# Layer 2 of a four-layer attention kernel: exponentials turned before they are normalised, the context product with tokens on partitions and a column of ones

## The chip, the core and the metric

One core of a Trainium2 chip. The time is the device time of one execution in microseconds (us). TensorE is PE (its weight loads are PEld), VectorE DVE, ScalarE ACT, GpSimd POOL.

## The reference

Four cross-attention layers follow each other on x and a context, both (32, 64, 256) in float32. The change is in layer 2, grouped-query attention with 32 query heads on 8 key/value heads of 8 features:

```
q = x @ Wq + bq ; k = ctx @ Wk + bk ; v = ctx @ Wv + bv      # 32 heads of q, 8 of k and v, HD = 8
attn = softmax(q @ k.T / sqrt(8) + mask)                      # (32 batches, 32 heads, 64, 64)
x = (attn @ v) @ Wo + bo + x                                  # then a layer norm
```

## The kernel before

2048 tokens are worked on as PAIRS = 16 pairs of batches, 128 tokens each. Layers 0 and 1 come first, then `phase_mlp_grouped_attention`: the MLP of layer 1 and, behind it, layer 2's attention, one pair after another. Layer 3 follows behind a barrier. Every engine has its own in-order queue, written out by hand as a loop over t in which several pairs are in flight; `there(p)` leaves out pairs that don't exist, and semaphores join the queues.

A pair's scores lie on 128 partitions (2 of the query heads times 64 query tokens), 2048 in each (16 heads, 2 batches, 64 keys), in two halves of 1024. Its way:

- PE `project(p)` (products through `accumulate`, L1322): queries, keys and values into one PSUM bank. ACT `move_projected` copies queries (L1493) and values (L1498), the latter into `v_bd`, which has zeros around them; DVE `place_keys` (L1577) spreads the keys.
- PE `scores(p)` (L1385). DVE `add_mask(p, half)`: scale and mask out of PSUM into `soft` (L1554), row maxima (L1561). POOL `subtract(p, half)` (L1282). ACT `exponent(p, half)` (L1479).
- DVE `invert(p, half)`: sums (L1565) and their reciprocals (L1570). POOL `normalize(p, half)` multiplies into `prob` (L1290, two instructions a half).
- PE `turn(p, half)`: 8 transposes into `t_ps` (L1398). `t_ps` has room for one half, so that the second half waits for ACT `move_turned(p, 0)` (L1483), which copies it to `pt`.
- PE `context(p)` (L1410): 16 products. `v_bd` is the stationary side with 32 columns, `pt` the moving side with 128; four products at a time go to the four column strips of the array. The result has features on partitions. ACT `move_context` (L1507).
- PE `outputs(p)`: two products with Wo (L1418) and one of a row of ones with the bias (L1419). DVE `add_output` (L1582) adds onto x.

A float32 product makes two weight-load and two matmul records in the trace, a transpose one of each. Queue orders of one step t: PE scores(t-1), project(t), context(t-3), turn(t-2, 0), outputs(t-3), turn(t-2, 1). ACT exponent(t-2, 1), move_projected(t), move_context(t-3), move_turned(t-2, 0), exponent(t-1, 0), move_turned(t-2, 1). At t = 2 also `turn_features(LAST)` (L1360, moved at L1474), which turns the last block of the MLP's result. The full orders are in the loops below.

Of the kernel before, what the change touches and what calls it, by code (L numbers as in the profile page):

```python
# [1203 lines left out]
def phase_mlp_grouped_attention(nc, A, G, w, b1, g, loads, loads3):  # L1204
# [14 lines left out]
    with Mem(nc, "mg", G.psum) as m:  # L1219
# [6 lines left out]
        cols, bv_wide, one = m.sb("cols", [P, 4]), m.sb("bv_wide", [P, P]), m.sb("one", [1, P])  # L1226
# [6 lines left out]
        rmax, rsum, rinv = (m.sb(n, [P, HALVES, 16]) for n in ("rmax", "rsum", "rinv"))  # L1233
# [5 lines left out]
        s_ps, t_ps = m.ps("s_ps", (P, TILES, 4, 2, T)), m.ps("t_ps", (P, 2, 2, 2, P))  # L1239
        p_bank, c_bank = m.ps("p_bank"), m.ps("c_bank")  # L1240
        hid_ps = [s_ps[:, n, :, :, :].rearrange("p v b t -> p (v b t)") for n in range(RING)]
        out_ps = [t_ps[:, n, :, :, :].rearrange("p b q n -> p (b q n)") for n in range(2)]
        q_ps, k_ps, v_ps = p_bank[:, 0:D].rearrange("p (c n) -> p c n", c=2), p_bank[:, D:D + P], p_bank[:, D + P:D + P + 64]
        c_ps, o_ps = c_bank[:, 0:D].rearrange("p (b c t) -> p b c t", b=2, c=2), c_bank[:, 0:D]
# [7 lines left out]
        zero_made, v_zero, folded_made, spread_made, one_made = (m.sem(n) for n in ("zero_made", "v_zero", "folded_made", "spread_made", "one_made"))  # L1252
# [3 lines left out]
        s_psum, masked, max_done, shifted, exp_done, sum_done, inv_done, prob_ready = (m.sem(n) for n in  # L1256
            ("s_psum", "masked", "max_done", "shifted", "exp_done", "sum_done", "inv_done", "prob_ready"))
        t_psum, pt_done, c_psum, ot_done, o_psum, x_done = (m.sem(n) for n in
            ("t_psum", "pt_done", "c_psum", "ot_done", "o_psum", "x_done"))

        def there(pair):
            return 0 <= pair < PAIRS
# [4 lines left out]
        with nc.Block() as block:  # L1267
# [10 lines left out]
            def _(pool):  # L1278
# [5 lines left out]
                def normalize(p, half):  # L1284
                    pool.wait_ge(inv_done, 2 * p + half + 1)
                    if p:
                        pool.wait_ge(t_psum, 2 * p + half - 1)
                    for n in range(2):
                        i = 2 * half + n
                        pool.tensor_tensor(prob[:, i, :, :, :].rearrange("p b v t -> p v b t"), soft[p % 2][half][:, n, :, :, :],  # L1290
                                           rinv[:, half, 8 * n:8 * n + 8].rearrange("p (v b) -> p v b", v=4).unsqueeze(3)
                                           .to_broadcast([P, 4, 2, T]), ALU.mult).then_inc(prob_ready, 1)
# [4 lines left out]
                pool.memset(v_bd[:, :, :, :, :], 0.0).then_inc(v_zero, 1)  # L1297
                pool.memset(one[:, :], 1.0).then_inc(one_made, 1)
# [9 lines left out]
                for t in range(PAIRS + 2):  # L1308
                    if there(t - 2):
                        normalize(t - 2, 0)  # L1310
                    if there(t - 1):
                        subtract(t - 1, 0)
                    if there(t - 2):
                        normalize(t - 2, 1)
                    if there(t - 1):
                        subtract(t - 1, 1)

            @block.tensor
            def _(pe):
# [43 lines left out]
                def project(p):  # L1363
# [25 lines left out]
                def turn(p, half):  # L1389
                    pe.wait_ge(prob_ready, 4 * p + 2 * half + 2)  # L1390
# [4 lines left out]
                    for n in range(2):  # L1395
                        for b in range(2):
                            for q in range(2):
                                mm = pe.transpose(t_ps[:, n, b, q, :],  # L1398
# [814 lines left out]
```

## Time and profile before

| | |
|---|---|
| median of 3 runs | 1658.1 us (1653.25 to 1659.24) |
| the profiled execution | 1658.67 us, its span 1656.9 us |
| busy: PE, PEld, DVE, ACT, POOL | 1541.7, 1321.7, 1102.9, 673.1, 451.4 us |
| scores of pair 0 and of pair 15 start | 1192.45 and 1325.93 us |

The span is from the first to the last instruction. Line numbers in the rows are those of the kernel before. A row of the timeline has start, duration (both us), engine, line, instruction, what it writes and reads, how many are merged, and in brackets the idle time ahead of it with what ended it.

### The profile page before, as it was taken

To read this page: it belongs to the slowest core of one execution; us is meant where nothing else is said; L and a number is where in the kernel's file an instruction comes from. 1 tells how busy PE (TensorE), PEld (TensorE's weight loads), DVE (VectorE), ACT (ScalarE), POOL (GpSimd) and SP (SyncE) were. 2 spreads that over 40 slices of the span, in tenths; PEclk is the share of its full clock that TensorE was granted. 3 is DMA by queue.
4 is the path that set the end of the run, shared out by engine and by line. 5 is a ranking of instruction groups with operands and counts; after the bars stand their busy time and mean duration, and the time that the engine had idled before them with its cause. 6 is when DMAs were issued, how large, how long until landed. Compare 5 with 4: busy or idle time off the path is not lost. (4 is left out here: it accounts for less than half of the span.)

```text
span 1656.9 us, 33073 instructions
## 1 busy us (share of the span) xinstructions
PE 1541.7 (93%) x13299; PEld 1321.7 (80%) x13299; DVE 1102.9 (67%) x2371; ACT 673.1 (41%) x1270; POOL 451.4 (27%) x532
## 2 busy tenths in 40 slices
PE   4987999999999999999999999879988859999799
PEld 2666888888888888888888888869867747888598
DVE  6886666666666676666666667555599945676444
ACT  4654434343333434433343434432366633544322
POOL 2004120020101211210200200232188866653211
PEclk9998999999999999999999999889989979999899
DMA  4000010010000000000100100020030000000000
GB/s 132 1 0 26 14 39 14 1 39 14 27 14 14 27 14 14 27 14 14 39 14 1 39 27 1 30 45 1 2 115 2 1 1 2 2 2 3 1 26 25
DMA packets 44580, 34.16 MB, mean 21 GB/s; under 512 B 10770, under 2 KB 41496, under 8 KB 44312
## 3 DMA queue, kind: packets, MB, share of 16 engines
q1 hardware_dynamic: 44440, 32.17, 6.7%
q8 instruction: 102, 1.67, 0.4%
q14 instruction: 38, 0.31, 0.1%
HBM read 30.00 MB, written 2.10 MB: 19 GB/s over the span
## 5 line engine op out<-in xcount | busy, mean ns | idle before, releaser
L946 DVE STREAM_TRANSPOSE att_pt<-att_prob 32x256 f32<-32x256 f32 x496 | 215.9, 435 | 6.4
L846 ACT ACTIVATE g_q_sb<-psum,g_cols 128x512 f32<-128x512 f32 x128 | 88.4, 690 | 321.0 <-PE psum L714 321.0
L763 PE MATMUL psum<-g_wo_hi,att_ot_hi 128*128 128x256 f32 x512 | 150.2, 293 | 2.5 <-DVE att_ot_lo L959 1.4
L917 DVE TENSOR_REDUCE att_rmax<-psum 128x6 f32<-128x390 f32 (+1 forms) x96 | 49.2, 512 | 151.3 <-PE psum L676 151.3
L763 PE MATMUL psum<-g_wo_lo,att_ot_hi 128*128 128x256 f32 x512 | 145.5, 284 | 0.0
L763 PE MATMUL psum<-g_wo_hi,att_ot_lo 128*128 128x256 f32 x512 | 145.4, 284 | 0.0
L746 PE MATMUL psum<-att_pt,att_v_sb 128*128 128x128 f32 x1024 | 128.9, 280 | 3.5 <-DVE att_ot_lo L959 3.5
L969 DVE TENSOR_TENSOR g_x_res<-psum,g_x_res 128x256 f32<-128x256 f32 x128 | 54.3, 424 | 116.8 <-PE psum L763 88.5
L746 PEld LDWEIGHTS psum<-att_pt,att_v_sb 128*128 128x128 f32 x1024 | 123.2, 194 | 7.8 <-DVE att_ot_lo L959 3.7
L849 ACT ACTIVATE att_k_sb<-psum,g_cols 128x512 f32<-128x512 f32 x128 | 88.2, 689 | 81.0 <-PE psum L714 81.0
L714 PE MATMUL psum<-split_feat_hi,g_wide_hi 128*128 128x512 f32 x256 | 103.7, 405 | 4.5 <-DVE split_feat_lo L993 3.3
L728 PE MATMUL psum<-g_wv_hi,split_ctx_hi 128*128 128x512 f32 x256 | 105.6, 413 | 0.0
L763 PEld LDWEIGHTS psum<-g_wo_hi,att_ot_hi 128*128 128x128 f32 x512 | 98.7, 193 | 5.1 <-DVE att_ot_lo L959 1.7
L714 PE MATMUL psum<-split_feat_lo,g_wide_hi 128*128 128x512 f32 x256 | 100.6, 393 | 0.0
L714 PE MATMUL psum<-split_feat_hi,g_wide_lo 128*128 128x512 f32 x256 | 100.4, 392 | 0.0
L763 PEld LDWEIGHTS psum<-g_wo_lo,att_ot_hi 128*128 128x128 f32 x512 | 98.8, 193 | 1.9
L728 PE MATMUL psum<-g_wv_hi,split_ctx_lo 128*128 128x512 f32 x256 | 100.0, 391 | 0.0
L728 PE MATMUL psum<-g_wv_lo,split_ctx_hi 128*128 128x512 f32 x256 | 99.9, 390 | 0.0
L829 ACT ACTIVATE att_ot_hi<-psum 128x512 fp32r<-128x512 f32 x128 | 73.3, 593 | 65.5 <-PE psum L746 65.5
L714 PE MATMUL psum<-split_ctx_hi,g_wide_hi 128*128 128x512 f32 x256 | 99.9, 390 | 0.0
L714 PE MATMUL psum<-split_ctx_lo,g_wide_hi 128*128 128x512 f32 x256 | 99.8, 390 | 0.0
L714 PE MATMUL psum<-split_ctx_hi,g_wide_lo 128*128 128x512 f32 x256 | 99.8, 390 | 0.0
(301 smaller groups left out, 3936.5 us busy)
## 6 DMA issues: line engine op xcount, KB each, us to landing
g_ctx_f<-in_L_xattn_wq SPq DMA_DIRECT2D x32, 128.0 KB, 2.3
g_ctx_f<-in_L_xattn_wk SPq DMA_DIRECT2D x32, 128.0 KB, 2.8
g_ctx_f<-in_L_xattn_wv SPq DMA_DIRECT2D x8, 512.0 KB, 3.8
g_ctx_f<-in_L_xattn_wo SPq DMA_DIRECT2D x8, 512.0 KB, 3.8
c_ctx_tok<-in_ctx SPq DMA_DIRECT2D x4, 512.0 KB, 5.5
g_x_res<-in_x SPq DMA_DIRECT2D x4, 512.0 KB, 8.7
g_w<-in_L_xattn_mlp_w SPq DMA_DIRECT2D x2, 1024.0 KB
out<-g_x_res SPq DMA_DIRECT2D x8, 256.0 KB, 2.2
```

Source lines behind the costliest of these rows:

```text
L714: mm = pe.matmul(dst[:, :], a, b_, start=(k == 0 and t == 0), stop=(k == KT - 1 and t == 2))
L728: mm = pe.matmul(v_ps[p % 2][:, :], a, b, start=(k == 0 and t == 0), stop=(k == KT - 1 and t == 2))
L746: mm = pe.matmul(c_ps[:, p % 2, h, :], v_sb[:, p, h * K1:(h + 1) * K1], pt[:, h, pp, p % 2, :, :].rearrange("p u t -> p (u t)"), start=Tru ...
L763: mm = pe.matmul(o_ps[p % 2], a, b, start=(h == 0 and t == 0), stop=(not last and h == HG - 1 and t == 2))
L829: act.activation(ot_hi[:, p, :, :], c_ps[:, p % 2, :, :], ACT.Copy).then_inc(ot_high, 1)
L846: act.activation(q_sb[:, h, :], q_ps[:, :], ACT.Identity, bias=G.cols[:, layer, head:head + 1]).then_inc(q_ready, 1)
L849: act.activation(k_sb[:, h, :, 0:T], k_ps[:, :].rearrange("p (b t) -> p b t", t=T), ACT.Identity, bias=G.cols[:, layer, H1 + head:H1 + hea ...
L917: dve.tensor_reduce(rmax[:, a:b], s_ps[group][:, :, :], X_AXIS, ALU.max).then_inc(max_done, 1)
L946: turned = dve.transpose(pt[to:to + 32, :, :, r, u, 32 * a:32 * a + 32].rearrange("p h a t -> p (h a) t"), by_pair[of:of + 32, :, u, 32 * ...
L969: dve.tensor_tensor(G.x_res[:, pair, :], o_ps[p % 2], G.x_res[:, pair, :], ALU.add).then_inc(x_added, 1)
```

## The change

The division by the sums moves from the 2048 probabilities of a partition to the 256 context values. `exponent` is followed by `turn` directly. `context(p)` has `pt` (128 columns) as the stationary side and as the moving side the values of both batches with a column of ones behind each, 2 x 9 = 18 columns; 16 products, none side by side in the array, with query tokens on partitions. DVE `normalize` inverts the sums (columns 8) and multiplies while it leaves PSUM; `turn_context` turns the result so that features are on partitions; `outputs` has two products, and POOL adds the bias onto x beforehand. `prob`, `one`, the sums' instructions and POOL's multiplications go. Context moves a step earlier, behind `turn(t-2, 1)`, and outputs last. The same in short:

```diff
-    v_bd = m.sb("v_bd", [P, 4, 2, 2, 2 * ROWS])
-    prob = m.sb("prob", [P, TILES, 2, 4, T])
+    v_bd = m.sb("v_bd", [P, 4, 8, 2, HD + 1])
+    ctx_n = m.sb("ctx_n", [P, 2, 16, HD])
...
-    c_ps, o_ps = c_bank[:, 0:D].rearrange("p (b c t) -> p b c t", b=2, c=2), c_bank[:, 0:D]
+    c_ps = c_bank[:, 0:2 * 16 * (HD + 1)].rearrange("p (b h d) -> p b h d", b=2, h=16)
+    ct_ps, o_ps = c_bank[:, 0:D].rearrange("p (b c t) -> p b c t", b=2, c=2), p_bank[:, 0:D]
...
+            def add_bias(p):
+                pool.tensor_tensor(G.x_res[:, p, :], G.x_res[:, p, :], g.o_bias[:, :], ALU.add).then_inc(bias_added, 1)
...
+            pool.wait_ge(bias_done, 1)
+            pool.wait_ge(f_psum, KT * NBLK)
+            pool.wait_ge(mlp_done, 2 * NBLK)
+            for p in range(PAIRS):
+                subtract(p, 0)
+                add_bias(p)
+                subtract(p, 1)
...
                 if p:
                     pe.wait_ge(k_done, p)
+                if p >= 4:
+                    pe.wait_ge(x_done, p - 3)
...
             def turn(p, half):
-                pe.wait_ge(prob_ready, 4 * p + 2 * half + 2)
+                pe.wait_ge(exp_done, 2 * p + half + 1)
...
+                    for v in range(4):
+                        mm = pe.transpose(t_ps[:, n, v, :], soft[p % 2][half][:, n, v, :, :].rearrange("p b t -> p (b t)"), G.ident[:, :])

             def context(p):
                 pe.wait_ge(pt_done, 2 * p + 2)
                 pe.wait_ge(v_done, p + 1)
                 if p:
-                    pe.wait_ge(x_done, p)
+                    pe.wait_ge(ot_done, p)
+                for i in range(TILES):
+                    for v in range(4):
+                        mm = pe.matmul(c_ps[:, :, 4 * i + v, :], pt[:, p % 2, i, v, :], v_bd[:, p % 4, 4 * (i % 2) + v, :, :],
+                                       start=True, stop=True)
+                mm.then_inc(c_psum, 1)
+
+            def turn_context(p):
+                pe.wait_ge(norm_done, p + 1)
                 for b in range(2):
+                    mm = pe.transpose(ct_ps[:, b, :, :].rearrange("p c t -> p (c t)"), ctx_n[:, b, :, :].rearrange("p h d -> p (h d)"), G.ident[:, :])
+                mm.then_inc(ct_psum, 1)
 
             def outputs(p):
                 pe.wait_ge(ot_done, p + 1)
-                for c in range(2):
-                    pe.matmul(o_ps, ot[:, c, :], g.wo[:, c, :], start=(c == 0), stop=False)
-                pe.matmul(o_ps, one[:, :], g.o_bias[0:1, :], start=False, stop=True).then_inc(o_psum, 1)
+                pe.wait_ge(k_done, min(p + 4, PAIRS))
+                accumulate(o_ps, [(ot[:, c, :], g.wo[:, c, :]) for c in range(KT)]).then_inc(o_psum, 1)
...
-                if there(t - 3):
-                    context(t - 3)
                 if there(t - 2):
                     turn(t - 2, 0)
                 if there(t - 3):
-                    outputs(t - 3)
+                    turn_context(t - 3)
                 if there(t - 2):
                     turn(t - 2, 1)
+                    context(t - 2)
+                if there(t - 3):
+                    outputs(t - 3)
...
             def move_turned(p, half):
                 act.wait_ge(t_psum, 2 * p + half + 1)
+                if p >= 2:
+                    act.wait_ge(c_psum, p - 1)
+                act.activation(pt[:, p % 2, tiles(half), :, :].rearrange("p i v n -> p (i v n)"),
+                               t_ps[:, :, :, :].rearrange("p i v n -> p (i v n)"), ACT.Copy).then_inc(pt_done, 1)
...
                 for b in range(2):
-                    for u in range(2):
-                        a = act.activation(
-                            v_bd[T * u:T * u + T, p % 4, b, :, :].rearrange("p h (q x) -> p h q x", x=16)[:, :, 0:4:3, 8 * u:8 * u + 8],
-                            v_ps[T * b:T * b + T, :].rearrange("p (h q u d) -> p h q u d", h=2, q=2, u=2)[:, :, :, u, :], ACT.Copy)
+                    a = act.activation(v_bd[T * b:T * b + T, p % 4, :, b, 0:HD],
+                                       v_ps[T * b:T * b + T, :].rearrange("p (h d) -> p h d", h=8), ACT.Copy)
...
                 if t == 2:
                     move_features(LAST)
+                if there(t - 2):
+                    move_turned(t - 2, 0)
                 if there(t - 3):
                     move_context(t - 3)
-                if there(t - 2):
-                    move_turned(t - 2, 0)
                 if there(t - 1):
                     exponent(t - 1, 0)
                 if there(t - 2):
...
-                    dve.wait_ge(prob_ready, 4 * (p - 2) + 2 * half + 2)
+                    dve.wait_ge(t_psum, 2 * (p - 2) + half + 1)
...
+            def normalize(p):
+                dve.wait_ge(c_psum, p + 1)
                 if p:
+                    dve.wait_ge(ct_psum, p)
+                dve.reciprocal(rinv[:, :, :], c_ps[:, :, :, HD]).then_inc(inv_done, 1)
+                dve.wait_ge(inv_done, p + 1)
+                dve.tensor_tensor(ctx_n[:, :, :, :], c_ps[:, :, :, 0:HD], rinv[:, :, :].unsqueeze(3).to_broadcast([P, 2, 16, HD]),
+                                  ALU.mult).then_inc(norm_done, 1)
...
             def add_output(p):
                 dve.wait_ge(o_psum, p + 1)
+                dve.wait_ge(bias_added, p + 1)
                 dve.tensor_tensor(G.x_res[:, p, :], o_ps, G.x_res[:, p, :], ALU.add).then_inc(x_done, 1)
...
             for t in range(1, PAIRS + 3):
+                if there(t - 3):
+                    normalize(t - 3)
                 if there(t - 1):
                     add_mask(t - 1, 0)
-                if there(t - 2):
-                    invert(t - 2, 1)
-                if there(t - 1):
                     add_mask(t - 1, 1)
                 if t == 1:
                     add_block(LAST)
                 if t >= 2 and there(t):
                     place_keys(t)
-                if there(t - 1):
-                    invert(t - 1, 0)
                 if there(t - 3):
                     add_output(t - 3)
```

## Rows read from the trace of the kernel before

**Rows 1.** The page, part 1: busy time and share of the span.
```profile
PE 1541.7 (93%) x13299; PEld 1321.7 (80%) x13299; DVE 1102.9 (67%) x2371; ACT 673.1 (41%) x1270; POOL 451.4 (27%) x532
```
**Rows 2.** Busy time by stretch, layer 2's attention: stretch, length, engines, clock share, DMA.
```profile
1209.50:1325.90 116.40, 104.93 (x1119) 83.20 (x1118) 108.78 (x129) 72.73 (x143) 100.76 (x78) 0.95 0.08 23
1325.90:1348.10 22.20, 16.03 (x163) 11.64 (x162) 11.13 (x16) 9.22 (x11) 12.67 (x11) 0.85 0.01 2
1272.60:1307.70 35.10, 30.72 (x349) 24.36 (x348) 33.82 (x41) 22.38 (x44) 31.33 (x25) 1.00 0.01 2
```
**Rows 3.** Timeline, one step of the loop at full clock.
```profile
1245.90 1.15 PE L1385 MATMUL psum<-mg_k_bd,mg_q_sb 32*128 32x256 f32 x16
1246.97 1.16 PE L1322 MATMUL psum<-split_feat_f,mg_wq 128*128 128x128 f32 x8
1247.11 1.23 DVE L1554 SCALAR_TENSOR_TENSOR split_soft<-psum,mg_mask 128x1024 f32<-128x1024 f32 x1 [0.18 <-PE psum L1385]
1248.37 1.22 DVE L1561 TENSOR_REDUCE mg_rmax<-split_soft 128x16 f32<-128x1024 f32 x1
1248.90 1.08 PE L1410 MATMUL psum<-split_pt,mg_v_bd 128*32 128x128 f32 x32
1249.67 1.90 POOL L1282 TENSOR_TENSOR split_soft<-split_soft,mg_rmax 128x1024 f32<-128x1024 f32 x1 [0.90 <-DVE mg_rmax L1561]
1249.91 1.09 PE L1398 MATMUL psum<-g_ident,mg_prob 128*128 128x128 f32 x8
1250.84 1.07 PE L1418 MATMUL psum<-g_wo,mg_ot 128*128 128x256 f32 x4
1251.84 0.69 PE L1419 MATMUL psum<-g_o_bias,mg_one 1*128 1x256 f32 x2
1253.63 1.09 PE L1398 MATMUL psum<-g_ident,mg_prob 128*128 128x128 f32 x8 [1.10 <-POOL mg_prob L1290]
```
**Rows 4.** Timeline, a turn at half clock, its move and the exponentials behind it.
```profile
1204.13 1.94 PE L1398 MATMUL psum<-g_ident,mg_prob 128*128 128x128 f32 x8 [2.68 <-ACT split_feat_f L1474]
1206.11 1.02 ACT L1483 ACTIVATE split_pt<-psum 128x1024 f32<-128x1024 f32 x1 [2.12 <-PE psum L1398]
1207.03 1.05 ACT L1479 ACTIVATE split_soft<-split_soft 128x1024 f32<-128x1024 f32 x1
```
**Rows 5.** Weight loads and narrow products, by line and in the timeline.
```profile
L1901 PEld LDWEIGHTS psum<-l_v_one,l_pt x1024: 132/138/138, 1385.6 to 1547.8; 128*64 128x64 f32 x171
L1418 PEld LDWEIGHTS psum<-g_wo,mg_ot x64: 186/190/337, 1215.0 to 1346.4; 128*128 128x128 f32 x64
...
1248.31 0.53 PEld L1322 LDWEIGHTS psum<-g_wkv,g_ctx_f 128*128 128x128 f32 x4
...
1406.76 2.00 PE L1901 MATMUL psum<-l_v_one,l_pt 128*64 128x17 f32 x64
```
**Rows 6.** By line: what goes, and layer 3's instructions of the kind that comes.
```profile
L1565 DVE TENSOR_REDUCE mg_rsum<-split_soft x32: 1206/1209/1221, 1199.7 to 1337.6; 128x16 f32<-128x1024 f32 x32
L1290 POOL TENSOR_TENSOR mg_prob<-split_soft,mg_rinv x64: 1042/1044/1047, 1201.3 to 1340.2; 128x512 f32<-128x512 f32 x64
L2036 DVE RECIPROCAL l_rinv<-psum x16: 246/248/258, 1388.8 to 1548.1; 128x16 f32<-128x16 f32 x16
L2040 DVE TENSOR_TENSOR l_ctx_n<-psum,l_rinv x16: 423/424/426, 1389.0 to 1548.4; 128x256 f32<-128x256 f32 x16
L1783 POOL TENSOR_TENSOR l_attn<-g_x_res,g_o_bias x16: 723/728/832, 1355.4 to 1497.9; 128x256 f32<-128x256 f32 x16
```
**Rows 7.** A stretch at half clock, by stretch and in the timeline.
```profile
1228.00:1231.00 3.00, 3.00 (x23) 2.26 (x16) 2.02 (x5) 1.73 (x2) 2.48 (x3) 0.50 0.00 0
...
1227.65 1.90 PE L1385 MATMUL psum<-mg_k_bd,mg_q_sb 32*128 32x256 f32 x16
1229.48 2.02 PE L1322 MATMUL psum<-split_feat_f,mg_wq 128*128 128x128 f32 x8
```
**Rows 8.** Timeline, the turn of the MLP's last block ahead of the loop.
```profile
1200.41 1.04 PE L1360 MATMUL psum<-g_ident,g_x_res 128*128 128x128 f32 x8
```

More of the change, by code:

```diff
@@ L1225, in phase_mlp_grouped_attention @@
         wq, wk = m.sb("wq", [P, KT, D]), m.sb("wk", [P, KT, P])
-        cols, bv_wide, one = m.sb("cols", [P, 4]), m.sb("bv_wide", [P, P]), m.sb("one", [1, P])
+        cols, bv_wide = m.sb("cols", [P, 4]), m.sb("bv_wide", [P, P])
         mask = m.sb("mask", [P, B, T])
@@ L1251, in phase_mlp_grouped_attention @@
         f_psum, f_moved = m.sem("f_psum"), m.sem("f_moved")
-        zero_made, v_zero, folded_made, spread_made, one_made = (m.sem(n) for n in ("zero_made", "v_zero", "folded_made", "spread_made", "one_made"))
+        zero_made, v_zero, v_ones, folded_made, spread_made = (m.sem(n) for n in ("zero_made", "v_zero", "v_ones", "folded_made", "spread_made"))
         w_ready, cols_psum, cols_done, bv_done, bias_psum, bias_done = (m.sem(n) for n in
@@ L1255, in phase_mlp_grouped_attention @@
         p_psum, q_done, v_done, k_done = (m.sem(n) for n in ("p_psum", "q_done", "v_done", "k_done"))
[L1256 to L1259, printed above, removed]
+        s_psum, masked, max_done, shifted, exp_done = (m.sem(n) for n in ("s_psum", "masked", "max_done", "shifted", "exp_done"))
+        t_psum, pt_done, c_psum, inv_done, norm_done, ct_psum, ot_done, bias_added, o_psum, x_done = (m.sem(n) for n in
+            ("t_psum", "pt_done", "c_psum", "inv_done", "norm_done", "ct_psum", "ot_done", "bias_added", "o_psum", "x_done"))
         def there(pair):
@@ L1296, in _ @@
                 pool.tensor_tensor(lo_w, raw_w, hi_w.bitcast(F32), ALU.subtract).then_inc(w2_ready[1], 1)
-                pool.memset(v_bd[:, :, :, :, :], 0.0).then_inc(v_zero, 1)
-                pool.memset(one[:, :], 1.0).then_inc(one_made, 1)
+                pool.memset(v_bd[:, :, :, :, :].rearrange("p r h b d -> p (r h b d)"), 0.0).then_inc(v_zero, 1)
+                pool.wait_ge(v_zero, 1)
+                for b in range(2):
+                    pool.memset(v_bd[T * b:T * b + T, :, :, b, HD:HD + 1].rearrange("p r h o -> p (r h) o"), 1.0).then_inc(v_ones, 1)
+                pool.wait_ge(v_ones, 2)
                 for n in range(NBLK * FT):
@@ L1395, in turn @@
                     for n in range(2):
-                        for b in range(2):
-                            for q in range(2):
-                                mm = pe.transpose(t_ps[:, n, b, q, :],
-                                                  prob[:, 2 * half + n, b, 2 * q:2 * q + 2, :].rearrange("p v t -> p (v t)"), G.ident[:, :])
+                        for v in range(4):
+                            mm = pe.transpose(t_ps[:, n, v, :], soft[p % 2][half][:, n, v, :, :].rearrange("p b t -> p (b t)"), G.ident[:, :])
                     mm.then_inc(t_psum, 1)
@@ L1482, in move_turned @@
                     act.wait_ge(t_psum, 2 * p + half + 1)
-                    act.activation(pt[:, p % 2, tiles(half), :, :, :].rearrange("p i b q n -> p (i b q n)"),
-                                   t_ps[:, :, :, :, :].rearrange("p i b q n -> p (i b q n)"), ACT.Copy).then_inc(pt_done, 1)
+                    if p >= 2:
+                        act.wait_ge(c_psum, p - 1)
+                    act.activation(pt[:, p % 2, tiles(half), :, :].rearrange("p i v n -> p (i v n)"),
+                                   t_ps[:, :, :, :].rearrange("p i v n -> p (i v n)"), ACT.Copy).then_inc(pt_done, 1)
                 def move_projected(p):
```

46 lines of the change are left out of this document (7 added, 39 removed).

## The prediction

> **What bounds the kernel now.** I read the page's busy shares first: PE 93% of the span [rows 1], an average over four layers that says nothing of layer 2. So I took the busy times by stretch for the attention loop of layer 2. From the scores of pair 2 (1209.5) to those of pair 15 (1325.9) it makes 13 steps in 116.4 us, 8.95 us each; in four steps at full clock (35.1 us) a step takes 8.78, with DVE busy for 33.82 / 4 = 8.46, POOL 7.83, PE 7.68, ACT 5.60 [rows 2]. DVE is the bound, and POOL is close. The timeline of one step shows the same: DVE is idle 0.18 us ahead of the mask, while PE stands 1.10 us for POOL's normalised half before the second turn [rows 3]. The stage is 8% of the kernel; the edit can't touch the rest.
>
> PE's own work in a step, from start to start [rows 3]: scores 1.07, projections 1.93 (1246.97 to 1248.90), context 1.01, first turn 0.93, outputs 1.00, row of ones 0.69, second turn about 0.95.
>
> **What goes and comes off PE.** DVE loses two sums of 1.21 and two reciprocals of about 0.25, 2.92 us a pair, and gets a reciprocal (0.25) and a product out of PSUM (0.42): -2.25. POOL loses 4 x 1.04 = 4.18 and gets one addition of 0.73: -3.45 [rows 6]. ACT writes the values in two instructions for four; nearly nothing. With that DVE would have 6.2 us of work a step and POOL 4.4. Were they still the bound, this would be the gain.
>
> **Context.** This is the term that decides. Before, 32 records with 128 moving columns run four abreast and take 1.01 us, 0.032 each [rows 3]. After, they are 32 loads of 128 columns with 18 moving columns, none abreast. No row has just that, but the values' product has 128 loaded columns and 64 moving: its four loads last 0.53 in all with 0.19 for the last, so they start 0.113 apart [rows 5]. The moving side is half as long as in the keys' product and the pace no better, so the load sets it. The length of a load says so too: 138 ns with 64 columns and 190 with 128, 52 ns for 64 columns, 104 for 128 [rows 5]. I take 0.113: 32 x 0.113 = 3.6 us, 2.6 more than before. Lower bound: layer 3's 64 records of 64 loaded and 17 moving columns, two abreast, in 2.00 us, 0.0625 for each strip, so 2.0 us [rows 5]. Upper bound: the same 32 at half clock, 7.2.
>
> A rule of the Trainium skill speaks against this edit. TensorEngine Tiling (Array Packing), Performance Considerations, advises to swap stationary and streaming sides where the streaming side has at most 32 columns, and to run four column tiles. The kernel before has that form and the edit undoes it; by the page's factor of four the context would take up to 4 x 1.01 = 4.0 us, near my 3.6, and a step would be 0.4 longer at full clock.
>
> Rest of PE: the ones (0.69) go, two transposes of 0.12 come. Without a wait a step would need 1.07 + 1.93 + 0.93 + 0.24 + 0.95 + 3.6 + 1.0 = 9.7 us, already over 8.95.
>
> **The new order adds two waits.** `t_ps` holds one half, and what lay between the two turns (outputs and ones, 1.69) is now 0.24. Behind the second turn comes its own context at once. The second turn's move on ACT is queued behind exponent(t-1, 0), which needs the scores made at the start of the very same step. So there is a closed chain from the scores to the next scores, all in PE's order:
> - scores to mask 1.21, mask to maxima 1.26, maxima to POOL 1.30 [rows 3];
> - POOL's subtraction 1.90 + 0.05 to hand over [rows 3];
> - exponential to the next ACT start about 0.95 (move to exponential is 0.92), move 1.02 + 0.08 [rows 4]: 7.74 us to the start of context;
> - context 3.6, outputs 1.0: 12.3 us a step.
>
> The second turn is ready sooner: the projections end at 3.0, first turn to move 1.13, move 1.10, second turn from 5.2 to 6.2. PE stands about 1.0 us ahead of it and 1.5 ahead of context. Both stalls are new; the 1.10 for POOL goes. Queued behind context are outputs and the next scores, and for these wait DVE's next mask and all after it.
>
> The other waits cost nothing in the loop. `project` waits for the addition onto x of four pairs back, outputs for keys that DVE places by about 6.8 into the step, `move_turned` for a context one step old, `normalize` for a context that ended 1.0 us before the step. The moved `normalize` (0.67) and `add_output` (0.36) lie in the first 1.2 us of the step, before the mask can start. The bias addition lies on POOL between two subtractions, with 12.3 - 4.5 us of room; without that cover it would cost 0.73 a step. The setting of zeros and ones in `v_bd` lies in the MLP, where POOL waits.
>
> **The clock.** Of the loop's 116.4 us the granted clock is 0.95 on average [rows 2]. It is at 1.2 GHz, half, in the stretch 1228 to 1231, right behind the ones, the 1.10 us idle and a turn; there scores take 1.83 for 1.07 [rows 7], and a turn at half clock 1.94 for 1.09 [rows 3, 4]. In the new step PE has from 3.0 to 7.7 nothing but two turns, one small turn and 2.5 us of idle time, more of that kind than stood ahead of 1228, and behind it a context that streams 18 columns for each 128 loaded. So I expect the clock to fall in most steps, ahead of or in context, and to come back in scores or projections. A step with context, outputs and scores at half clock: scores to mask 1.9 in place of 1.21, so 8.43 to context, + 7.2 + 2.0 = 17.6 us. In part of the steps it will fall only within context; I take four fifths of the way: 12.3 + 0.8 x 5.3 = 16.5 us. Ends: 12.3 (never), 20.8 (always: projections also at half, then 5.4 + 2 x (1.98 + 1.10) = 11.6 to context, + 9.2).
>
> **Start.** POOL now waits before its first subtraction for the turn of the MLP's last block, 1200.41 + 1.04 = 1201.45 [rows 8]. Two subtractions and a bias (4.55), an exponential (1.05) and ACT's moves of projections and features (2.1) put the first turn at about 1209.3, against 1204.13 [rows 4]. Two turns with moves (4.5 at full, 6.2 at half clock) and context(0), which now lies before scores(2): 1217.4 or 1222.7 against 1209.5, +7.9 or +13.2. I take +12.
>
> **End.** From the scores of pair 15 to the barrier it was 22.2 us [rows 2]. Now a step, two turns with moves, context, outputs, addition, inversion and product, a turn, ACT's move, outputs and addition: 12.3 + 4.5 + 3.6 + 1.0 + 1.1 + 0.3 + 0.5 + 1.1 + 0.4 = 24.8, at half clock 37.5: +2.6 or +15.3. I take +13.
>
> **Sum.** 13 x (16.5 - 8.95) = +98, +12, +13: +123 us. On the profiled execution's own 1658.67 us (span 1656.9 and 1.8 around it) that is 1782 us. The median of the runs is 0.6 lower, so nothing changes: I say 1781.
>
> **Rivals.**
> - *The clock stays up.* For it: layer 3's context with 17 columns runs at full clock in its loop. Against it: there it is 2.0 us long and wide products stand right before and behind it. 13 x (12.3 - 8.95) = 43.6, + 7.9 + 2.6: 1713 us. Chance 0.14.
> - *Narrow products are cheaper than the load row says.* For it: 0.0625 for each strip [rows 5]. Context 2.0, at half clock 4.0: steps of 10.7 and 14.4, at four fifths 13.7; 13 x 4.75 = 62, + 9 + 8: 1737 us, and 1688 with the clock up. Against it: those loads have half the columns. Chance 0.10.
>   The Trainium skill, TensorEngine Tiling, Instruction Overhead, says that a product with one moving column costs as much as one with 60, some 60 cycles; alone that would make the context 0.8 us and, at full clock, the step 9.5 and the kernel about 1670. No row here has a 128-column product at such a pace, so it has part of that 0.10 only.
> - *Half clock throughout.* 13 x 11.85 = 154, + 13.2 + 15.3: 1841 us. For it: context is over a third of the step. Against it: outputs, scores and projections follow each other without a gap, and in rows like those of 1228 to 1231 such work brought the clock back. Chance 0.10.
> - *Faster: DVE's relief is what counts.* If context hid behind the other work and the chain did not close, a step would be PE's 7.1 us: 13 x (7.1 - 8.95) = -24, + 8 at the start: 1643 us. It decides at context below 8.95 - 7.74 - 1.0 = 0.2 us a pair, or with ACT's move free of the exponential and context at 1.0. For it speaks only that DVE and POOL are the bound today. Chance 0.03; with no change in between 0.02.
>
> **Numbers.** Forecast 0.61. A difference under 0.5%, 8 us, can't be told from none here. Slower 0.61 + 0.14 + 0.10 + 0.10 = 0.95. Range 1700 to 1830: it takes in the clock staying up, part of the cheap loads and part of the way to 1841.
>
> **What would show it.** Scores 16 to 17 us apart in the loop; PE's context records 0.11 us apart at full clock and 0.22 at half; PE idle about 1.0 ahead of the second turn and 1.5 ahead of context, ended by ACT's moves; DVE and POOL idle for half of each step, the mask waiting for scores; first subtraction at 1201.5. I am wrong if context takes 2 us or less, if the granted clock is over 0.9 in the loop, or if the second turn's move starts before the exponential of the next pair.

## The result and the profile after

| | median of the runs, us | lowest to highest, us |
|---|---|---|
| before | 1658.5 (4 runs) | 1653.3 to 1659.2 |
| after | 1784.4 (4 runs) | 1783.2 to 1785.4 |

The changed kernel is slower: ratio 1.0764, interval [1.0743, 1.0784], against a forecast of 1781 us. The profiled execution has a span of 1783.8 us, 126.9 more than before. The page's first part answers to [rows 1]. The busy time of DVE and POOL fell, and PE's rose by 99.7 us with the same count of matmul records:

```profile
PE 1641.4 (92%) x13299; PEld 1419.3 (80%) x13299; DVE 1071.2 (60%) x2339; ACT 667.6 (37%) x1238; POOL 397.6 (22%) x485
```

The busy times by stretch answer to [rows 2]. The columns are the stretch, its length, then busy time of PE, weight loads, DVE, ACT and POOL with their counts, the granted clock as a share of 2.4 GHz, and DMA. In order: scores of pair 0 to those of pair 2; twelve steps of the loop; scores of pair 15 to the barrier; the rest of the kernel (layer 3).

```profile
1190.59:1220.59 30.00, 18.99 (x129) 17.11 (x129) 11.99 (x12) 8.65 (x13) 8.84 (x6) 0.68 0.51 159
1237.40:1442.87 205.47, 175.46 (x1033) 154.14 (x1032) 78.80 (x96) 63.34 (x108) 53.35 (x36) 0.70 0.00 1
1442.87:1476.20 33.33, 24.54 (x131) 20.44 (x130) 8.55 (x14) 7.03 (x9) 4.44 (x3) 0.70 0.00 0
1476.20:1783.80 307.60, 276.51 (x3509) 238.94 (x3509) 173.95 (x380) 115.21 (x217) 125.48 (x230) 0.94 0.03 8
```

So a step went from 8.95 us at a clock of 0.95 [rows 2] to 205.47 / 12 = 17.12 at 0.70. DVE is busy for 6.6 us of it and POOL for 4.4, near what the prediction counted (6.2 and 4.4), and neither sets the step now. The whole difference of 126.9 is made up so: the loop's 13 steps 222.3 against 116.4, +105.9; the start, pair 0 to pair 2, 30.0 against 17.05, +12.9; the end 33.3 against 22.2, +11.1; the stages ahead of pair 0 -1.9 and layer 3 -1.2, neither of them touched by the change.

One step in the timeline (start, duration, engine, line, operation, and in brackets the idle time before it with what ended it) answers to [rows 3]:

```profile
1254.80 1.81 PE L1381 MATMUL psum<-mg_k_bd,mg_q_sb 32*128 32x256 f32 x16
1256.54 1.16 PE L1316 MATMUL psum<-split_feat_f,mg_wq 128*128 128x128 f32 x8
1256.69 1.23 DVE L1551 SCALAR_TENSOR_TENSOR split_soft<-psum,mg_mask 128x1024 f32<-128x1024 f32 x1 [0.63 <-PE psum L1381]
1258.37 1.04 PE L1393 MATMUL psum<-g_ident,split_soft 128*128 128x128 f32 x8
1259.25 1.90 POOL L1282 TENSOR_TENSOR split_soft<-split_soft,mg_rmax 128x1024 f32<-128x1024 f32 x1 [12.79 <-DVE mg_rmax L1558]
1260.74 1.06 PE L1393 MATMUL psum<-g_ident,split_soft 128*128 128x128 f32 x8 [1.10 <-ACT split_pt L1482]
1261.18 1.06 ACT L1476 ACTIVATE split_soft<-split_soft 128x1024 f32<-128x1024 f32 x1 [0.32 <-POOL split_soft L1282]
1262.14 1.01 ACT L1482 ACTIVATE split_pt<-psum 128x1024 f32<-128x1024 f32 x1
1263.20 7.01 PE L1403 MATMUL psum<-mg_v_bd,split_pt 128*128 128x18 f32 x32 [1.40 <-ACT split_pt L1482]
1270.05 2.05 PE L1316 MATMUL psum<-g_wo,mg_ot 128*128 128x256 f32 x4
1272.03 1.73 PE L1381 MATMUL psum<-mg_k_bd,mg_q_sb 32*128 32x256 f32 x16
1272.14 0.42 DVE L1580 TENSOR_TENSOR g_x_res<-psum,g_x_res 128x256 f32<-128x256 f32 x1 [9.93 <-PE psum L1316]
```

From the scores to the context it is 8.40 us, with most of the scores at half clock. The context takes 6.85 us from start to start, the outputs 1.98. The busy times by stretch for these two say that both run at 1.2 GHz throughout:

```profile
1263.20:1270.05 6.85, 6.85 (x33) 6.85 (x33) 0.00 (x0) 1.06 (x1) 0.49 (x1) 0.50 0.00 0
1270.05:1272.03 1.98, 1.98 (x5) 1.15 (x5) 0.00 (x0) 0.00 (x0) 0.00 (x0) 0.50 0.00 0
```

The clock comes back late in the scores (0.50 up to 1256.20, 1.00 behind it) and holds through projections and turns. It falls in PE's idle time ahead of the context: the granted clock is 1.00 from 1261.80 to 1262.50 and 0.88 from 1262.50 to 1263.20, on average.

### The profile page after: what moved, and what is told of

The parts are those of the page before. It is cut to its first block and busy times, and to the rows that moved or that the text cites. A ratio compares the mean times of both kernels' runs of the same rounds, so it can differ in the third digit from the quotient of the medians.

```text
span 1783.8 us, 32990 instructions
## 1 busy us (share of the span) xinstructions
PE 1641.4 (92%) x13299; PEld 1419.3 (80%) x13299; DVE 1071.2 (60%) x2339; ACT 667.6 (37%) x1238; POOL 397.6 (22%) x485
## 5 line engine op out<-in xcount | busy, mean ns | idle before, releaser
L1403 PE MATMUL psum<-mg_v_bd,split_pt 128*128 128x18 f32 x512 | 107.7, 370 | 23.5 <-ACT split_pt L1482 23.5
L1403 PEld LDWEIGHTS psum<-mg_v_bd,split_pt 128*128 128x128 f32 x512 | 105.9, 320 | 27.4 <-ACT split_pt L1482 27.4
L1282 POOL TENSOR_TENSOR split_soft<-split_soft,mg_rmax 128x1024 f32<-128x1024 f32 x32 | 60.8, 1901 | 195.0 <-DVE mg_rmax L1558 180.7
```

Of the source, the lines that this page charges most:

```text
L1282: pool.tensor_tensor(s, s, rmax[:, half, :].unsqueeze(2).to_broadcast([P, 16, T]), ALU.subtract).then_inc(shifted, 1)
L1403: mm = pe.matmul(c_ps[:, :, 4 * i + v, :], pt[:, p % 2, i, v, :], v_bd[:, p % 4, 4 * (i % 2) + v, :, :], start=True, stop=True)
```

## The experiments

Three things were added up in the forecast: a closed chain through PE's order, a context priced by its weight loads, and a clock that falls. The times of the runs without an interval are single ones, and what is read from these runs is read from their profiles. The kernel before took 1656.3 us beside e2 to e5, and 1653.8 to 1659.4 (median 1657.7) beside e6, e1, e8 and w1.

A single time is only good to some us, since untouched work moves too. Layer 3, the same in all of them, takes 307.5 to 311.1 us in ten of the eleven profiles and 314.3 in e5's, at a mean granted clock of 0.91 there for 0.94 in the changed kernel's. So the text also gives the length of layer 2's attention, from the scores of pair 0 to PE's first product behind the barrier: 155.9 us in the kernel before, 285.7 in the changed one.

In the next three, one moves the context's width, one PE's idle time, one both, so that with the changed kernel they make a square.

**Wide moving side (e2_wide).** Each of the context's 32 products streams 128 columns instead of 18; the additional ones land in columns of the bank that a later product overwrites or nobody reads. The order of heads and batches in that bank changes with it. The main lines of the edit:

```diff
-        v_bd = m.sb("v_bd", [P, 4, 8, 2, HD + 1])
+        v_bd = m.sb("v_bd", [P, 4, 15, 2, HD + 1])
...
-        c_ps = c_bank[:, 0:2 * 16 * (HD + 1)].rearrange("p (b h d) -> p b h d", b=2, h=16)
+        c_ps = c_bank[:, 0:2 * 16 * (HD + 1)].rearrange("p (h b d) -> p b h d", b=2, h=16)
...
-                            mm = pe.matmul(c_ps[:, :, 4 * i + v, :], pt[:, p % 2, i, v, :], v_bd[:, p % 4, 4 * (i % 2) + v, :, :],
+                            at, frm = 18 * (4 * i + v), 18 * (4 * (i % 2) + v)
+                            mm = pe.matmul(c_bank[:, at:at + 128], pt[:, p % 2, i, v, :],
+                                           v_bd[:, p % 4, :, :, :].rearrange("p h b d -> p (h b d)")[:, frm:frm + 128],
...
```

Expected:

> The changed kernel with 128 moving columns in each of the 32 context records in place of 18 (the further columns land in columns that later products write over, so the loads are the same and the result too). Theory A, loads set the pace and the clock falls in the stretch of turns and idle time ahead of context and is then kept down by the narrow columns: context records stay 0.11 us apart at full clock, the clock still falls ahead of context but comes back inside it, step 13.7 to 14.5 us for 17.1, about 1740 us. Rival, the narrow columns alone bring the clock down: step 12.3, about 1715. Rival, the idle time alone does: step 16 to 17, 1770 to 1784. If the moving columns set the pace at all, the context gets longer.

Measured: 1734.3 us (attention 231.3), though the context streams seven times the columns. The timeline of the step in which the clock was down longest:

```profile
1304.71 1.06 PE L1393 MATMUL psum<-g_ident,split_soft 128*128 128x128 f32 x8 [1.09 <-ACT split_pt L1484]
1307.17 6.79 PE L1404 MATMUL psum<-mg_v_bd,split_pt 128*128 128x128 f32 x32 [1.40 <-ACT split_pt L1484]
1313.80 1.03 PE L1316 MATMUL psum<-g_wo,mg_ot 128*128 128x256 f32 x4
```

and by stretch, from the second turn to the context and from there to the outputs:

```profile
1304.71:1307.17 2.46, 1.06 (x8) 0.82 (x8) 1.47 (x2) 2.10 (x3) 2.46 (x3) 0.88 0.01 3
1307.17:1313.80 6.63, 6.63 (x33) 6.63 (x33) 0.00 (x0) 1.06 (x1) 0.49 (x1) 0.53 0.01 2
```

The clock still falls ahead of most contexts, in the idle time, but comes back within them, in this step near the end and in others sooner (most contexts take 5.2 to 5.5 us). Outputs and scores are at full clock again (1.03 for 2.05). In four of the thirteen steps the clock does not fall at all, with the same idle time. Steps are 12.4 to 15.3 us, 13.5 on average.

**Idle time filled (e3_fill).** Products thrown away, three ahead of the second turn and four ahead of the context, into a bank that is free there. Each streams 224 columns, so that the edit adds wide products as well as taking idle time away.

```diff
+                def fill(p, n):
+                    pe.wait_ge(masked, 2 * p + 1)
+                    for _ in range(n):
+                        pe.matmul(s_ps[:, 0, :, :, :].rearrange("p v b t -> p (v b t)")[:, 0:224], wq[:, 0, 0:P], feat_f[:, 0, 0:224], start=True, stop=True)
...
+                        if there(t - 1):
+                            fill(t - 1, 3)
                         turn(t - 2, 1)
+                        if there(t - 1):
+                            fill(t - 1, 4)
                         context(t - 2)
```

Expected:

> The changed kernel with float32 products of 128 x 224 that are thrown away in PE's two gaps: 3 ahead of the second turn, 4 ahead of context (0.37 us each at full clock), so that PE works on while it would wait. Theory A: the clock is up when context starts and falls inside or behind it, because the columns are narrow; step 13.5 to 17, 1725 to 1780. Rival, idle time alone brings it down: step 12.4, about 1716. Rival, what is in the gaps is irrelevant and the narrow columns alone count: step as now, 17.1, or longer by the fill.

Measured: 1737.1 us (attention 239.5), steps of 13.9 on average. This is the other half of the effect. The context starts at full clock. In most steps it also ends so (3.64 to 3.75 us in 12 of 16), and the clock falls in the outputs behind it. In the step below it falls towards the end of the context. Either way what follows pays.

```profile
1307.14 4.42 PE L1403 MATMUL psum<-mg_v_bd,split_pt 128*128 128x18 f32 x32
1311.40 2.05 PE L1316 MATMUL psum<-g_wo,mg_ot 128*128 128x256 f32 x4
1313.38 2.09 PE L1381 MATMUL psum<-mg_k_bd,mg_q_sb 32*128 32x256 f32 x16
```

**Both (e4_wide_fill).** The two edits above together.

Expected:

> Both: 128 moving columns in context and thrown-away products in the two gaps. Theory A: full clock throughout, the step is the bare chain at full clock, 12.3 to 12.5 us, 13 x 4.7 = 61 and some 15 at the ends less than 1784: about 1713. Rival, the clock is lost for another reason (transposes, loads): step over 14, over 1735.

Measured: 1711.2 us (attention 213.3). The timeline of one step:

```profile
1289.63 1.15 PE L1381 MATMUL psum<-mg_k_bd,mg_q_sb 32*128 32x256 f32 x16
...
1297.36 3.84 PE L1404 MATMUL psum<-mg_v_bd,split_pt 128*128 128x128 f32 x32
1301.04 1.03 PE L1316 MATMUL psum<-g_wo,mg_ot 128*128 128x256 f32 x4
1301.99 1.15 PE L1381 MATMUL psum<-mg_k_bd,mg_q_sb 32*128 32x256 f32 x16
```

and the stretch around it:

```profile
1222.00:1340.00 118.00, 118.00 (x959) 105.98 (x957) 59.71 (x76) 49.65 (x84) 41.72 (x28) 1.00 0.01 1
```

Scores to context 7.73 us, context 3.68, outputs 0.95: a step of 12.36, every step. That is the prediction's sum for full clock (7.74 + 3.6 + 1.0 = 12.3) term by term, and the kernel's time is near that of its rival with a clock that stays up (1713). The square, by step and granted clock in the loop:

| | idle as it is | idle filled |
|---|---|---|
| 18 columns | 17.1 us, 0.70 | 13.9 us, 0.87 |
| 128 columns | 13.5 us, 0.91 | 12.4 us, 1.00 |

Either edit alone takes back 3.2 or 3.6 of the 4.7 us that half clock costs a step. Neither the idle time nor the narrow context alone brings the changed kernel's 0.70. That it is the lost idle time, and not the 224 columns of the fill, which helps in e3 and e4 is not shown by the square; the next two runs have no idle time and no fill.

**The same work in another order (e5_covered).** Context moves one step later, between the two turns; the small turn goes behind the scores, the outputs last, one pair later still. No instruction is added or left out; ACT's and DVE's orders and three waits follow suit.

```diff
...
+                    if there(t - 4):
+                        turn_context(t - 4)
...
-                        turn_context(t - 3)
+                        context(t - 3)
                     if there(t - 2):
                         turn(t - 2, 1)
-                        context(t - 2)
-                    if there(t - 3):
-                        outputs(t - 3)
+                    if there(t - 4):
+                        outputs(t - 4)
...
```

Expected:

> The changed kernel in another order, with the same instructions: context(t-3) between the two turns, turn_context(t-4) behind the scores, outputs(t-4) last, ACT's and DVE's orders to match. Nothing waits for ACT's moves, so that the step is PE's own work: 9.7 to 9.9 us at full clock. Theory A: no gap, but the narrow columns remain; if the clock stays up about 1685 us, and if narrow columns and turns alone bring it down, a step of 12 to 14, 1710 to 1735. If the wide loads were not the floor (the stalls being all of the cost), the step would be 8.9 or less and the kernel at or under 1665.

Measured: 1701.9 us (attention 195.2), steps of 9.3 to 12.1, 11.2 on average: less than the 12 to 14 expected for a clock that narrow columns bring down, more than the 9.7 to 9.9 for one that stays up. The waits are gone, and the clock falls all the same. The stretch reads:

```profile
1222.00:1340.00 118.00, 118.00 (x915) 105.61 (x913) 70.53 (x84) 57.68 (x98) 45.53 (x31) 0.83 0.01 1
```

PE is busy for 118.00 of 118.00 us and granted 0.83, so that its busy share does not tell the clock here. A context that begins at full clock, in the timeline:

```profile
1293.72 3.64 PE L1403 MATMUL psum<-mg_v_bd,split_pt 128*128 128x18 f32 x32
1297.22 1.73 PE L1393 MATMUL psum<-g_ident,split_soft 128*128 128x128 f32 x8
```

The turn behind it takes 1.73 us for 1.04: the clock falls there.

**That order with the wide side (e6_covered_wide).** The edits of e5 and of e2 together.

Expected:

> The covered order of e5 with 128 moving columns in context: no gap and no narrow column, the same 32 loads of 128 columns. Theory A: full clock throughout and a step that is PE's own work, 9.7 to 9.9 us; 13 x 0.85 = 11 more than before, some 10 at both ends: about 1678. What it has over the kernel before is then the price of the loads alone. Rival, the loads could be hidden by a better order: step 8.95 or less.

Measured: 1668.7 us (attention 167.3). The stretch:

```profile
1222.00:1340.00 118.00, 118.00 (x1090) 108.81 (x1091) 84.38 (x100) 67.84 (x112) 55.32 (x38) 1.00 0.01 1
```

A context in the timeline, up to the turn behind it:

```profile
1291.41 3.74 PE L1404 MATMUL psum<-mg_v_bd,split_pt 128*128 128x128 f32 x32
1294.99 1.04 PE L1393 MATMUL psum<-g_ident,split_soft 128*128 128x128 f32 x8
```

Between e5 and e6 only the context's moving columns differ (and the order of its columns in the bank), and the clock goes from 0.83 to 1.00 and the step from 11.2 to 9.37. This is the cleanest evidence for the narrow columns: no idle time and no fill in either. The turns are in both, so that turns alone, without idle time or narrow products, do not bring the clock down. The step of PE's own work is 0.35 below the prediction's 9.7, and the kernel 9 below the 1678 expected: projections take 1.73 for 1.93, and turns, context and outputs are each a little shorter. Here the 32 products take 3.58 us, 0.112 each with 128 columns; in e5 (1293.72 to 1297.22) 3.50, 0.109 each with 18. The moving side costs next to nothing beside a load of 128 columns. The two runs show that it hardly matters whether 18 or 128 columns move; that the load is the price follows with the narrow products of 64 loaded columns, 0.0625 for each strip [rows 5]. The Trainium skill (TensorE: Matmul & The Clock Gate, LDWEIGHTS (loading the stationary operand)) has a load last as long as its columns at 1.2 GHz, 107 ns for 128. The products' spacing at full clock, 109 to 112 ns, agrees; at half clock it is 214.

**ACT's order (e1_act_order).** In the changed kernel, the second turn's move ahead of the next pair's exponential. That takes the exponential out of the chain that the prediction wrote down.

```diff
+                    if there(t - 2):
+                        move_turned(t - 2, 1)
                     if there(t - 1):
                         exponent(t - 1, 0)
-                    if there(t - 2):
-                        move_turned(t - 2, 1)
```

Expected:

> The changed kernel with ACT's move of the second turn ahead of the next pair's first exponential, one line group moved. The prediction held that exponential for the last link of the closed chain; but the second turn waits for the first turn's move in any case and ends at 6.2 us of the step, so that its move can start 0.3 to 0.5 us sooner only. Theory A: step 16.6 to 17.1 for 17.1, 1777 to 1784. Rival, the exponential is the link that counts: step 14 or less at the unchanged clock pattern, under 1745.

Measured: 1784.6 us (attention 283.2), steps of 16.8. ACT now waits for the turn, where the turn's move waited for ACT, and little changes:

```profile
1258.41 1.06 PE L1393 MATMUL psum<-g_ident,split_soft 128*128 128x128 f32 x8 [1.09 <-ACT split_pt L1482]
1259.51 1.02 ACT L1482 ACTIVATE split_pt<-psum 128x1024 f32<-128x1024 f32 x1 [0.97 <-PE psum L1393]
1260.59 6.77 PE L1403 MATMUL psum<-mg_v_bd,split_pt 128*128 128x18 f32 x32 [1.11 <-ACT split_pt L1482]
```

The idle time ahead of the context goes from 1.40 to 1.11. Behind the chain through mask, subtraction and exponential lies another, only 0.3 us shorter: projections, turn, move, turn, move, context, with one `t_ps` for both halves. The loop is 3.6 us shorter (218.7 for 222.3). Layer 3, untouched, takes 311.1 us in this profile for 307.6, which hides it in the total.

**The start (e8_start).** POOL's three waits for the MLP's end go behind the first subtraction of pair 1, and the bias is added one pair late.

```diff
-                pool.wait_ge(bias_done, 1)
-                pool.wait_ge(f_psum, KT * NBLK)
-                pool.wait_ge(mlp_done, 2 * NBLK)
                 for p in range(PAIRS):
                     subtract(p, 0)
-                    add_bias(p)
+                    if p == 1:
+                        pool.wait_ge(bias_done, 1)
+                        pool.wait_ge(f_psum, KT * NBLK)
+                        pool.wait_ge(mlp_done, 2 * NBLK)
+                    if p:
+                        add_bias(p - 1)
...
```

Expected:

> The changed kernel with POOL's three waits (bias, turn of the MLP's last block, block added) behind the first pair's subtraction and the bias additions one pair late. Theory A: first subtraction some 5 us sooner, first turn some 5 us sooner, and the scores of pair 2 come 5 us earlier: 1778 to 1780. Rival, the first turn waits for ACT's moves of the MLP's last block anyway: no change within 1.5 us.

Measured: 1776.7 us, 7.7 less (attention 278.7). POOL's first subtraction, at 1199.81 in the changed kernel, and the first turn:

```profile
1192.66 1.90 POOL L1282 TENSOR_TENSOR split_soft<-split_soft,mg_rmax 128x1024 f32<-128x1024 f32 x1 [9.00 <-DVE mg_rmax L1561]
1200.08 1.94 PE L1396 MATMUL psum<-g_ident,split_soft 128*128 128x128 f32 x8 [2.33 <-ACT split_feat_f L1474]
```

The first turn starts 11.3 us behind the scores of pair 0, in the changed kernel 16.9 (1190.59 to 1207.45, and PE idle 7.87 ahead of it); pair 0 to pair 2 takes 24.5 us for 30.0. So 5.5 of the start's 12.9 are POOL's waits. The rest lies behind the first turn, where turns (1.94 us) and the context of pair 0 (7.01) run at half clock ahead of the scores of pair 2, in both the changed kernel and e8. The profiled span is 8.8 us shorter (1775.0 for 1783.8): besides the 5.5 it is 1.8 ahead of pair 0, which no edit touched, and 1.4 in the loop, where the contexts of pairs 1 to 4 take 5.6 to 5.9 us instead of 7.0 and the steps 16.8.

**Sums on PE, strips kept (w1_ones_product).** Can the normalisation leave DVE and POOL without the new layout? From the kernel before: the context keeps its four strips of 32 columns, a second set of such products against a block of ones gives each sum in every row that needs it, and DVE inverts 128x256 of them and multiplies as the context leaves PSUM. POOL only subtracts and adds the bias.

```diff
...
+                    for b in range(2):
+                        for q in range(2):
+                            for i in range(TILES):
+                                mm = pe.matmul(n_ps[ROWS * i:ROWS * (i + 1), b, :, :].rearrange("p c t -> p (c t)"),
+                                               ones[:, ROWS * q:ROWS * (q + 1)], pt[:, p % 2, i, b, q, :], start=(q == 0), stop=(q == 1))
...
+                    dve.reciprocal(rinv[:, :], c_bank[:, D:2 * D]).then_inc(inv_done, 1)
...
+                    dve.tensor_tensor(ot[:, :, :].rearrange("p c (b t) -> p b c t", b=2), c_ps, rinv[:, :].rearrange("p (b c t) -> p b c t", b=2, c=2),
+                                      ALU.mult).then_inc(ot_done, 1)
...
```

Expected:

> A version of its own, from the kernel before: the context product keeps its four narrow strips (values stationary with 32 columns), and a second set of 16 such products with a block of ones as the stationary side gives each feature's partition the sum that belongs to it. DVE inverts 256 sums a partition and multiplies while the context leaves PSUM; no turn of the context. ACT's exponentials write the order that the turns need (two instructions a half). Bias addition on POOL, a pair late; order scores, projections, turn, context, turn, outputs. Theory A: PE's own work is 1.07 + 1.93 + 0.93 + 2.0 + 0.95 + 1.0 = 7.9 us, DVE's about 6.5, POOL's 4.5; step 8.1 to 8.3 for 8.95, 13 x 0.75 = 10 us less: 1645 to 1650. Rival, the clock falls more often since more of PE's records are short: step 9 or more, no gain. Rival, an inversion of 256 elements out of PSUM costs DVE over 1 us and holds up outputs: 8.6, about 1655.

Measured: 1661.2 us (median of eleven runs), ratio to the kernel before 1.0023 [1.0014, 1.0033]: no gain, where 1645 to 1650 was expected. The timeline of a step:

```profile
1266.40 1.06 PE L1414 MATMUL psum<-split_pt,mg_ones 128*32 128x128 f32 x32
1267.62 1.75 DVE L1561 RECIPROCAL mg_rinv<-psum 128x256 f32<-128x256 f32 x1
1269.74 0.74 DVE L1573 SCALAR_TENSOR_TENSOR mg_k_bd<-psum,mg_cols,mg_spread 128x512 f32<-128x512 f32 x1
1269.88 1.13 PE L1320 MATMUL psum<-g_wo,mg_ot 128*128 128x256 f32 x4 [1.40 <-DVE mg_ot L1565]
```

The sums cost PE 0.99 us, but the inversion takes 1.75 on DVE, and PE waits for its result. Keys for the next scores stand behind it in DVE's queue. This is the second rival named beforehand, and it costs more than was put on it: a step takes 9.32 and not 8.6. The first rival is out, since the granted clock is 1.00 in four such steps (1261.62 to 1298.88).

**The same, ordered (w2_ones_ordered).** DVE places the keys ahead of the inversion and adds the output between its two maskings; PE issues the outputs behind the next step's projections.

```diff
...
                     if there(t):
                         project(t)
...
+                    if there(t - 4):
+                        outputs(t - 4)
...
-                    if there(t - 3):
-                        normalize(t - 3)
                     if t >= 2 and there(t):
                         place_keys(t)
                     if there(t - 3):
-                        add_output(t - 3)
+                        normalize(t - 3)
...
```

Expected:

> w1_ones_product with two orders changed: TensorE issues the output product of a pair behind the next step's scores and projections instead of last, and VectorE places the keys ahead of the inversion and adds the output between its two maskings. w1's step of 9.32 us was a chain: sum products, inversion 1.75, multiply 0.42, keys 0.74, scores, first masking, with TensorE idle 1.40 ahead of the output product and 0 to 0.5 elsewhere, and VectorE idle 0.68 and 0.56. Theory (the step is VectorE's chain and not TensorE's nor the clock's): without the two idles VectorE's own work sets the step, 2 x 1.23 + 2 x 1.22 + 1.75 + 0.42 + 0.74 + 0.42 = 8.23, less the overlap of neighbouring rows as the trace shows it, 8.1 to 8.2; TensorE's work is 7.8, it stays busy for 0.95 of the step and keeps the full clock, 1.00. Thirteen steps give 13 x 1.15 = 15 us back: 1646 us, 1642 to 1652, faster than the kernel before (ratio 0.993). Rival (the idle of TensorE was only the visible end of another loop, POOL's subtractions or ACT's moves, whose order was not changed): step 8.5 to 9.3 and 1650 to 1661. Rival (the half clock comes with any stretch of narrow products that fills TensorE): clock below 0.97 and over 1665.

Measured: 1640.2 us (four runs, 1640.0 to 1640.2), ratio 0.9895 [0.9875, 0.9914]: about 1% faster than the kernel before, whose fastest run beside it took 1653.0. The timeline:

```profile
1266.93 0.74 DVE L1573 SCALAR_TENSOR_TENSOR mg_k_bd<-psum,mg_cols,mg_spread 128x512 f32<-128x512 f32 x1
1267.59 1.74 DVE L1561 RECIPROCAL mg_rinv<-psum 128x256 f32<-128x256 f32 x1
1267.77 1.15 PE L1383 MATMUL psum<-mg_k_bd,mg_q_sb 32*128 32x256 f32 x16
1269.36 0.42 DVE L1565 TENSOR_TENSOR mg_ot<-psum,mg_rinv 128x256 f32<-128x256 f32 x1
1269.70 1.21 DVE L1550 SCALAR_TENSOR_TENSOR split_soft<-psum,mg_mask 128x1024 f32<-128x1024 f32 x1
1270.68 1.08 PE L1320 MATMUL psum<-g_wo,mg_ot 128*128 128x256 f32 x4
```

and by stretch, five steps:

```profile
1259.89:1299.28 39.39, 39.22 (x580) 33.73 (x581) 38.88 (x41) 28.13 (x60) 22.48 (x16) 1.00 0.01 2
```

A step takes 39.39 / 5 = 7.88 us, at full clock, with DVE busy for 7.78 and PE for 7.84 of it. The expected 8.1 to 8.2 counted too little overlap between neighbouring rows of DVE; the forecast of 1646, 1642 to 1652, was 6 us too high and its range missed by 2. Most of the gain over the kernel before lies in the loop: 102.1 us for 116.4. The attention as a whole takes 141.8 for 155.9; the stages ahead of it, untouched, were 3.3 us shorter in this profile (1189.13 for 1192.45). Reordering the kernel before could not have reached this step, since DVE alone has 8.46 us of work in each of its steps [rows 2].

## Why the prediction was right

The sign, the size and the three places hold, and so does the mechanism: the chain, the price of the loads and the clock were each found where they were put. That the total came within 4 us of 1784.4 is in part luck. The loop was put 8 us too low; the end was put 2 us too high, and the untouched stages happened to be 3 us shorter in the profiled execution. Point by point:

- *The bound.* DVE and POOL lost about the work that was counted, and after it the mask waits for PE's scores. DVE has 6.6 us a step where 6.2 was put; a part of the difference is its reciprocal, which takes 0.35 for 32 columns where the prediction had the 0.25 of 16.
- *Context at 0.113 a record.* 0.109 to 0.115 at full clock (e5, e6, e4), 0.214 at half. The cheap price (0.0625, from loads of half the columns) is ruled out for loads of 128 columns. So is the pace that the Trainium skill (TensorEngine Tiling (Array Packing), Instruction Overhead) gives to narrow moving sides, by which the prediction estimated 0.8 us for the context. The skill's advice on column tiles (TensorEngine Tiling (Array Packing), Performance Considerations), which speaks for the kernel before, is borne out: 3.5 us at full clock for 1.01 [rows 3], where its factor of four gives up to 4.0.
- *The closed chain.* 7.74 us at full clock (its terms as printed add up to 7.77), measured 7.73 in e4; 8.43 with the scores at half, measured 8.40. PE is idle for 1.10 and 1.40 where 1.0 and 1.5 were expected. That the exponential is what closes it was true but nearly beside the point: e1 takes it out and finds the next chain 0.3 us behind.
- *The clock.* A step with context, outputs and scores at half was put at 17.6 and took 17.1: the context, 0.214 a record, came out 0.35 under 7.2, and only part of the scores is at half. The share was mis-sized. "Four fifths of the way" stood for steps in which the clock falls only within the context; that was so in one step, the first of the loop (a context of 5.25 us). From then on it fell ahead of the context every time. So the step was 17.1 and not 16.5, and the loop +105.9 where the sum has +98. The four fifths were a judgement that no row gave. The two causes named (idle time with turns only, 18 columns for each 128 loaded) are both real; each alone takes 1.1 to 1.5 us a step (e2, e3 against e4), and together 4.7, more than their sum. The prediction named them as one thing and could not have priced them apart.
- *Start* +12, measured +12.9. The first turn was put at 1209.3; it came at 1207.45 in an execution that was 1.9 us earlier by then, so just where it was put. *End* +13, measured +11.1: the context of the last pair but one ran at half clock, that of the last partly at full (4.30 us).

With the experiments the difference can be split by what each takes away. It is taken from the length of layer 2's attention, which leaves out how the other stages moved. From 285.7 us to 213.3 (e4), 72 us, is the half clock. From 213.3 to 167.3 (e6), 46 us, is the closed chain. The last 11 us over the kernel before (155.9) are the loads of the context with what lies at both ends; the loop has 5.5 of them (9.37 a step for 8.95). By the kernels' whole times the three are 73, 42 and 10. All of these come from single profiles, and the middle one from kernels that differ in the fill as well as in the order.

What stays open is why 17.1 us is so regular, why four steps of e2 kept the clock with the same idle time as the others, and how far idle time and narrow products each must go before it falls. The runs show where it fell, not the rule.

## What to carry to other kernels

Work taken off the engine that bounds a stage can be worth nothing if the new layout gives up column strips on TensorE, as here. Price each product by its load as well as by its stream, and look at what is left between a turn and the next use of its bank. Look at the granted clock of the stretch after every such change; in e5 a PE that was never idle lost it, and a context at half clock took 6.85 us for 3.5. The idea behind the change, to normalise late, was sound once the sums were made in strips too and the queue of the bounding engine was put in order: 1640 us.

## What the runs showed of the hardware

- At one order and one count of instructions, with PE busy for 118.00 of 118.00 us, the granted clock was 0.83 with 18 moving columns in the context and 1.00 with 128 (e5, e6). More streaming made layer 2's attention 28 us faster (195.2 to 167.3) and the kernel 33 (1701.9 to 1668.7); 5 of these lie in layer 3, where no line differs, at a mean clock of 0.91 for 0.94.
- Products that nobody reads, of 224 moving columns each and put where PE was idle for 2.5 us a step, made the kernel 47 us faster (e3, 1737.1 for 1784.4).
- An inversion out of PSUM took 1.75 us for 128x256, 0.35 for 128x32 in the changed kernel and 0.25 for 128x16 [rows 6]: 6.2 ns for each further column. A product of the same size takes 0.42. Where the sums are replicated so that a plain multiply can use them, 256 of them a partition are inverted; the changed kernel inverts 32.
